# A gated product put ahead of the output turns, one shared last-chunk wait, and a softmax norm put ahead of a low part

## What is computed

```
x = x + mixer(layernorm(x))        # a linear recurrence over time, then a 256x256 projection
x = x + xattn(ctx, ctx, layernorm(x))   # 16 heads of 16, 64 keys, softmax(q k / 4) v, projection
x = x + ffn(layernorm(x))
ffn(x): h = silu(x W1 * s1) * (x W2 * s2)   # 256 -> 1024, gated
        h = gelu(h H1 * t1)                 # 1024 -> 1024
        h = gelu(h H2 * t2)                 # 1024 -> 1024
        return h W3 * s3                    # 1024 -> 256
```

## Time and profile before

| what | value |
|---|---|
| median of 3 runs | 993.42 us |
| the profiled execution | 998.99 us |
| its span, first to last instruction | 997.3 us |
| TensorE matmuls busy | 880.0 us, 88% |
| VectorE / ScalarE / GpSimd busy | 521.8 / 503.8 / 192.4 us |
| mean granted TensorE clock | 0.956 of full speed |

### The profile page before, as it was taken

One profiled execution on the slowest core, in us unless ns is written; L12 is line 12 of the kernel. 1 busy time (PEld: TensorE's weight loads), 2 busy tenths in 40 slices (PEclk: granted clock), 3 DMA queues, 4 the chain that ended last, 5 costly groups with the idle time before them and its releaser, 6 DMA issues.

```text
span 997.3 us, 15115 instructions
## 1 busy us (share of the span) xinstructions
PE 880.0 (88%) x5570; PEld 699.7 (70%) x5570; DVE 521.8 (52%) x891; ACT 503.8 (51%) x784; POOL 192.4 (19%) x207
## 2 busy tenths in 40 slices
PE   2035999559999999999999999999999999999996
PEld 0035877347787778777877787778777877787884
DVE  7972657335464546454645464546454545453421
ACT  2863544126635663566356635663566356635431
POOL 0773830032002200220032003200320032003000
PEclk9557999869999999999999999999999999999998
DMA  9896192520002000200010001000100010001000
GB/s 288 242 380 222 38 357 87 202 78 1 2 21 69 0 0 21 68 0 0 21 68 0 0 21 68 0 0 22 67 0 0 22 67 0 0 21 42 1 1 23
DMA packets 14631, 62.81 MB, mean 63 GB/s; under 512 B 2739, under 2 KB 4406, under 8 KB 13782
## 3 DMA queue, kind: packets, MB, share of 16 engines
q1 hardware_dynamic: 13862, 60.19, 17.4%
q10 hardware_dynamic: 704, 2.16, 0.8%
q0 software_dynamic: 32, 0.00, 0.0%
HBM read 50.16 MB, written 23.72 MB: 74 GB/s over the span
## 4 chain that ended last, share of the span: by engine, by line
PE 73%; DVE 9%; issue 6%; ACT 6%; DMA 3%; DVEq 0%; ACTq 0%; POOL 0%; SPq 0%; POOLq 0%
PE pair L1171 45%; PE pair L1158 10%; PE pair L1107 3%; PE pair L1096 3%; PE pair L1123 2%; ACT tok L285 2%; PE pair L471 2%; PE pair L478 2%; DMA x_rows<-x1t 1%; PE pair L1116 1%; PE pair L485 1%; PE pair L1063 1%; DVE red L923 1%; PE pair L538 1%; DVE vbuf L988 1%
## 5 line engine op out<-in xcount | busy, mean ns | idle before, releaser
L794 ACT ACTIVATE vbuf<-pair,scl 128x512 f32<-128x512 f32 x128 | 87.8, 686 | 237.1 <-PE pair L1171 231.3
L1171 PE MATMUL pair<-h1hi,h_turned 128*128 128x512 f32 x512 | 203.9, 398 | 1.5 <-DVE h1lo L959 1.5
L1171 PE MATMUL pair<-h2hi,h_turned 128*128 128x512 f32 x512 | 202.6, 396 | 0.0
L1171 PE MATMUL pair<-h1lo,h_turned 128*128 128x512 f32 x512 | 199.8, 390 | 0.0
L1171 PE MATMUL pair<-h2lo,h_turned 128*128 128x512 f32 x512 | 199.6, 390 | 0.0
L959 DVE TENSOR_TENSOR h1lo<-vbuf,h1hi 128x512 fp32r<-128x512 f32 x80 | 57.7, 721 | 119.5 <-ACT h1hi L795 118.7
L1171 PEld LDWEIGHTS pair<-h1hi,h_turned 128*128 128x128 f32 x512 | 96.1, 188 | 34.3 <-issue 10.5
L1158 PE MATMUL pair<-zThi,w_turned 128*128 128x512 f32 x224 | 92.4, 412 | 24.3 <-DVE vbuf L988 24.3
L1171 PEld LDWEIGHTS pair<-h2hi,h_turned 128*128 128x128 f32 x512 | 96.1, 188 | 25.2 <-issue 5.9
L1171 PEld LDWEIGHTS pair<-h2lo,h_turned 128*128 128x128 f32 x512 | 96.2, 188 | 19.3
L1171 PEld LDWEIGHTS pair<-h1lo,h_turned 128*128 128x128 f32 x512 | 96.2, 188 | 18.9
(11 more groups left out here) (142 smaller groups left out, 1503.9 us busy)
## 6 DMA issues: line engine op xcount, KB each, us to landing
h_turned<-d_h SPq DMA_DIRECT2D x2, 4096.0 KB, 13.6
tok<-in_xs SPq DMA_DIRECT2D x8, 512.0 KB, 6.9
EE<-alpha_rows SPq DMA_DIRECT2D x16, 256.0 KB, 10.1
xres<-in_x SPq DMA_DIRECT2D x8, 512.0 KB, 10.4
x_rows<-x1t SPq DMA_DIRECT2D x8, 512.0 KB, 2.6
xr<-x_rows SPq DMA_DIRECT2D x8, 512.0 KB, 3.5
out<-xr SPq DMA_DIRECT2D x8, 512.0 KB, 2.6
x_rows<-xres SPq DMA_DIRECT2D x7, 512.0 KB, 2.7
```

The lines of the kernel that those rows point to most:

```text
L794: e.activation(vb[:, s % 2, :], h_ps[s % 4], ACT.Gelu, scale=sc)
L1171: ins = e.matmul(bank, w[:, k, m * P:(m + 1) * P], src[part][:, k, :], start=(k == 0 and part == 0), stop=(k == HC - 1 and part == 1))
```

## The change

Three edits, in the code of ScalarE, VectorE and TensorE:

1. TensorE issues `gated_first(j)` of the next block behind `last(i, 1)`, ahead of `turn_out(i)`; its second half waits for the second output copy. The gate of that product is issued by VectorE behind `z_lo(j)`, ahead of the output addition and so ahead of the next body's `stats`. The output halves are copied into `prob` instead of `sg`. For block 0 both stand ahead of the loop.
2. The first two H1 products are issued together (`hidden_first`): chunks 0 to 6 of the first, chunks 0 to 6 of the second, then chunk 7 of the first and of the second.
3. The softmax norm of the first unit (`normalised(j, 0)`) is issued by VectorE ahead of the low part of hidden product 0 instead of behind it.

```diff
         def out_evac(i, m):
             e.wait_ge(S["mm"], 26 * i + (25 + m))
-            e.activation(sg[:, m, :], h_ps[m], ACT.Copy, scale=sc3[:, m:m + 1]).then_inc(S["o_ev"], 1)
+            e.activation(prob[:, m, :], h_ps[m], ACT.Copy, scale=sc3[:, m:m + 1]).then_inc(S["o_ev"], 1)
...
+        def gate(i, m):
+            e.wait_ge(S["sg_rdy"], 8 * i + (m + 1))
+            e.wait_ge(S["lo"], 24 * i + max(m - 1, 0))
+            e.scalar_tensor_tensor(vb[:, m % 2, :], pair[m % 2][:, 512:1024], sc2[:, m:m + 1], sg[:, m % 2, :],
+                                   ALU.mult, ALU.mult).then_inc(S["v_rdy"], 1)
+
         def body(i, attn):
             j = i + 1
             if attn:
                 e.wait_ge(S["x1_in"], 16 * j)
                 stats(2 * j)
-            for m in range(HC):
...
+            for m in range(1, HC):
+                gate(i, m)
...
             for s in range(2 * HC):
+                if attn and s == 0:
+                    normalised(j, 0)
                 low(i, HC + s, h2 if s < HC else h1)
...
-                if attn and s + 2 in TURN:
+                if attn and s > 0 and s + 2 in TURN:
                     normalised(j, TURN.index(s + 2))
...
             if attn:
                 z_lo(j)
+                gate(j, 0)
             e.wait_ge(S["o_t"], i + 1)
...
         def gated_first(i):
             e.wait_ge(S["z_hi"], DH * i + DH)
-            e.wait_ge(S["o_ev"], 2 * i)
             for g, w in enumerate((w1T, w2T)):
+                if not isinstance(i, int):
+                    e.wait_ge(S["o_ev"], 2 * i - (1 - g))
                 for part in range(2):
...
+        def hidden_first(i):
+            e.wait_ge(S["v_rdy"], 8 * i + 7)
+            for ks in (range(HC - 1), (HC - 1,)):
+                for m in range(2):
+                    for k in ks:
+                        if m == 0:
+                            e.wait_ge(S["lo"], 24 * i + (k + 1))
+                        for part in range(2):
+                            ins = e.matmul(h_ps[m], h1T[:, k, m * P:(m + 1) * P], h1[part][:, k, :],
+                                           start=(k == 0 and part == 0), stop=(k == HC - 1 and part == 1))
+                    if k == HC - 1:
+                        ins.then_inc(S["mm"], 1)
...
             last(i, 1)
+            if attn:
+                gated_first(j)
             turn_out(i)
```

More of the change, by code:

```diff
@@ L1049, in _ @@
         x1_add(e, 7)
+        gate(0, 0)
         with e.Fori(0, NBLK - 1) as i:
@@ L1149, in gated @@
         def gated(i, m):
-            if m == 0:
-                gated_first(i)
-                return
             if m >= 2:
@@ L1173, in product @@
             ins.then_inc(S["mm"], 1)
+        def hidden_first(i):
[10 more added lines that the diff above has]
+                        ins.then_inc(S["mm"], 1)
         def hidden(i, s):
-            if s < 2:
-                e.wait_ge(S["v_rdy"], 8 * i + 7)
-            elif s < 4:
+            if s < 4:
                 e.wait_ge(S["v_rdy"], 8 * i + 8)
@@ L1191, in turn_out @@
                 for m in range(TPB):
-                    ins = e.transpose(pair[2][:, m * DM + k * P:m * DM + (k + 1) * P], sg[:, k, m * P:(m + 1) * P], ident[:, :])
+                    ins = e.transpose(pair[2][:, m * DM + k * P:m * DM + (k + 1) * P], prob[:, k, m * P:(m + 1) * P], ident[:, :])
             ins.then_inc(S["o_t"], 1)
@@ L1202, in body @@
                     scores(j, 0)
-            for s in range(2 * HC):
-                hidden(i, s)
+            hidden_first(i)
+            for s in range(1, 2 * HC):
+                if s > 1:
+                    hidden(i, s)
                 if attn and s in TURN:
@@ L1256, in _ @@
         e.wait_ge(m["w_in"], 64)
+        gated_first(0)
         with e.Fori(0, NBLK - 1) as i:
```

## The result

The changed kernel takes 998.77 us (median of 19 runs, 995.47 to 1003.19) against 995.49 us for the kernel before, run beside it (19 runs, 992.68 to 998.71). The ratio is 1.0032, 95% interval 1.0017 to 1.0046: 3.2 us slower, clear of zero and inside the 0.5% that was called no change. A second series of runs gave 1.003 (1.0014 to 1.0046).

The account below looks back on a forecast made before the run. TensorE's pauses were taken to bound the kernel. The terms -3.3 - 3.0 + 14.1 - 0.5 - 1.6 = +5.7 us, added to 993.42, gave 999.1 us, with 989 to 1004 as the 8-in-10 range.

Parts of the forecast that it names:

- The case taken as likeliest: At the block seam, two GpSimd low parts delay VectorE's normalising; 2.35 us lost per seam, 996 to 1002 us, chance 0.55.
- What bounds the kernel: Whole kernel: the chain of waits runs on TensorE for 73%, so only TensorE's pauses are worth much.
- Last-chunk wait: First H1 product: joint issue removes TensorE's wait for chunk 7's low part; gain 0.47 us per block, 3.3 us in all.
- early norm: First probability turn: the norm fits VectorE's idle time, so TensorE's wait goes; gain 0.43 us, 7 times, 3.0 us.
- The seam's chain: Between blocks: table load, Silu, gate 0, output addition, statistics, gate 1; TensorE stops 1.5 us ahead of product 3.
- The price of two low parts: Normalising beside two GpSimd low parts ends 2.31 + 1.29 us behind 613.73; six seams lose 14.1 us.
- Output turn: Seam into block 7, without statistics: the pause at the output turn goes, gain 0.5 us.
- Block 0: First block's 21.5 us stall: product 2 runs inside it, saving eight matmuls at the slow clock; gain 1.6 us (1.2 to 2.0).
- One low part: Rival at the seam: only one GpSimd low part delays the normalising; 1.0 us per seam, 991.0 us, chance 0.13.
- or none: Rival at the seam: normalising isn't held up and takes 1.38 us; 0.25 us per seam, 986.5 us, chance 0.08.
- The falling clock: Rival: the new seam pauses also lower TensorE's clock; +3.4 to +10 us, 1002.5 to 1009 us, chance 0.12.
- The smaller stop: Rival: TensorE's stop at the seam is smaller than laid out; every 0.5 us is 3 us, 996 us, chance 0.08.

Follow-up runs that it names:

- the small edits alone: Kernel before with only the joint issue of the first two H1 products and the earlier softmax norm: ratio 0.9933, block period 98.67 us.
- the seam alone: Changed kernel with the joint H1 products and the earlier softmax norm undone, against the kernel before: ratio 1.011, block period 101.58 us.
- the kernel with the old seam and everything else moved: Changed kernel with early statistics and normalising, output-bias additions delayed, but output turns ahead of the next block's first gated product: ratio 0.9933 to the kernel before.
- the bias wait: Changed kernel with early statistics and normalising, plus GpSimd's output-bias additions waiting for low parts 6 and 7: ratio 0.9847 to the kernel before.
- the new order in block 0: Changed kernel with early statistics and normalising, delayed output-bias additions, and block 0's gate 1 ahead of the normalising: ratio 0.9826 to the kernel before.
- both low parts held back: Changed kernel with GpSimd's first two low parts waiting until the four normalising instructions are done: ratio 1.0014 to the kernel before.

## Why the prediction came out as it did

The forecast was 999.1 us, 5.7 more than the kernel before; measured were 998.77 and a difference of 3.2. The case taken as likeliest (two low parts in the way) is what the trace shows. The time lies in this case's own range of 996 to 1002; the chances split the result between slower and same, and it is same by the 0.5% line.

That the time was met within 0.3 us is luck. The forecast starts from 993.42, the median of three runs; over 19 runs the kernel before takes 995.49, and these 2.1 us hide a change that was forecast 2.5 us too large.

- *What bounds the kernel.* Right: only TensorE's pauses counted, and the period follows their sum.
- *Last-chunk wait and early norm.* 0.90 us a block forecast, 0.98 measured by the small edits alone (0.51 and 0.47, forecast 0.47 and 0.43). The first product's end, 2.8 us later, held nobody up.
- *The seam's chain.* Right to 0.1 us at each step. Set 5.35 us later, so that both scales begin at the end of the W3 products, the changed kernel has the moved gate at 608.58 (forecast 608.63), the addition at 609.25 (609.30), gate 1 at 612.58 (612.64), product 3 at 613.39 (613.43), and the normalising at 613.68 (613.73).
- *The price of two low parts.* The term that was mis-sized. For the second low part I added its whole length, 1.29, to the 2.31: 3.62 forecast, 3.30 measured. Each low part lengthens the four instructions by 0.96 only (1.38, 2.34, 3.30), and the earlier trace rows had this already: 0.40 became 1.37, which is 0.97. The seam lost 1.97 (rows) or 1.93 (the seam alone), not 2.35: 11.7 us in six seams instead of 14.1. These 2.4 us look like the whole error of the sum, but the other terms were not exact either: with 6.9 us for the small edits (forecast 6.3) and 1.7 or 2.5 for block 0 (1.6) the terms add up to +2.6 or +1.8, and 3.2 was timed. That gap lies inside the interval of the timed difference (1.7 to 4.6).
- *Output turn.* 0.5 forecast for the pause, 0.74 measured as its price, in the kernel with the old seam and everything else moved.
- *Block 0.* -1.6 forecast; -2.5 and -1.7 in the two pairs of profiles. It depends on when the granted clock rises after the restart: 6.0 us and 3.6 us in the two profiles of the kernel before, 4.4 and 2.9 in those of the changed kernel.
- *Rivals.* One low part, or none: both excluded by 2.58 us of low parts in a row and by the series 1.38, 2.34, 3.30. The falling clock: not seen. The granted clock was 1.00 from 603 to 613 in spite of pauses of 1.25 and 1.54 us, and it stayed there from block 0 to the last product. The smaller stop: not so either, since the chain came as laid out.

What the prediction did not ask is where the statistics could have gone. In the trace of the kernel before `z_lo` ends at 603.95, and the layout had the moved gate at 608.63, so 4.7 us in which VectorE has nothing to do could be read off:

```profile
602.66 1.29 DVE L954 TENSOR_TENSOR zTlo<-pair,zThi 128x512 fp32r<-128x512 f32 x2 [3.07 <-ACT zThi L774]
```

The kernel that puts statistics and normalising there is 1.4% faster than the kernel before (0.9857), with the bias wait and the new order in block 0 1.7% (0.9826; the two intervals overlap). It leaves TensorE's side of the first edit as it is.

## What to carry to other kernels

When an instruction is moved ahead in one queue, lay out every queue behind it: the moved gate was in time, but the output addition and the statistics behind it were not, although their queue stood idle just ahead of the gate. Look for work of the next pass that is ready by then and put it into that idle stretch. And where two engines block each other, count how many instructions of the one can be ready when the other starts, not how many were before: here the late power let a second low part pile up. Price each by what it added where it was seen, not by its own length.

## What the runs showed of the hardware

VectorE's four normalising instructions and GpSimd's low parts alternate one by one, at 0.96 us for each low part that gets in (1.38, 2.34, 3.30 us for the same four instructions). In the changed kernel the first two of the four take 1.38 and 1.36 us and the other two 0.40 each. A gate, which reads one input from PSUM, was not held up: it took its 0.75 us at 515.49 beside a low part that ran from 515.41 to 516.68 (both low parts held back). The Trainium skill, "SBUF — State Buffer" (section "Who interferes with whom"), has the blocking for a whole instruction, and the traces agree; the alternation is this case's. That the cause is a shared port no run here shows; the runs show the turns. Not expected was how far the phase matters: low parts 6 and 7 on VectorE take 1.47 us with GpSimd's four additions held back, and 1.82 or 2.39 us beside them, depending on which came first.

After the same stall of some 21 us, TensorE's granted clock rose from 0.50 to 1.00 6.0 us after the restart in one profile of the kernel before and 3.6 us in the other, and the stretch was 1.15 us shorter. Over the fourteen profiles of this case it was 2.9 to 6.0 us.
